# The last output tile of a gated cross-attention kernel, as one step of 288 rows or as two of 192 and 96

## The chip, the core and the metric

The kernel runs on one core of one Trainium2 chip. The metric is the device time of one execution in microseconds (us); the time of the kernel before is the median of three runs. A profile of one execution gives the rows that are read here. Its engines are PE (TensorE's matmuls), PEld (TensorE's weight loads), DVE (VectorE), ACT (ScalarE), POOL (GpSimd) and SP (SyncE, whose queue issues the DMAs).

## The reference

```python
# x (8, 100, 1024), memory (8, 722, 512), W_mem (1024, 512), W_gate (1024, 2048)
memory_proj = einsum('bme,de->bmd', memory, W_mem)
scores = einsum('bnd,bmd->bnm', x, memory_proj) / sqrt(1024)
attn = softmax(scores, axis=-1)
memory_context = einsum('bnm,bmd->bnd', attn, memory_proj)
gate_input = concatenate([x, memory_context], axis=-1)
gate = sigmoid(einsum('bnf,df->bnd', gate_input, W_gate) + b_gate)
fused = x + gate * memory_context
out = fused * rsqrt(mean(fused ** 2, axis=-1) + 1e-6) * norm_w
```

Eight batches of 100 rows make 800 rows of 1024 features. All is float32.

## The kernel before

Everything is kept with the feature on the partition and the row on the free axis, in eight tiles of 128 features (`KD` = 8). Products are made with fp32r operands split into a high and a low part: `three` (line 294) issues three matmuls for each pair of 128-feature tiles, high by high, low by high and high by low. Attention and the half of the gate product that needs only x come first. The stage that matters here is the last one: the gate product with the memory context, and what follows it.

That stage works through the list `STEPS`. A step is (output tile t, first row, end row): the first 512 rows of a tile (`FIRST`) or the last 288. The list runs the steps of 512 rows first, apart from one of 288 rows that stands third, and ends with seven steps of 288 rows, tiles 1 to 7. `END0` is the last step of 512 rows, `LAST` the last of all. For a step,

- PE runs `gate_mc(n)`: 8 input tiles by three matmuls into one of the PSUM banks 4 and 5 in turn. It first waits for the bank's seed, the x half of the gate product, which ACT writes there two steps ahead (`seed`);
- ACT takes the sigmoid with the bias (`sigmoid`, line 683), and in `finish` squares the fused tile (line 702) and multiplies it by norm_w (`weigh`, line 693);
- DVE multiplies by the memory context (`gate_times`, line 881), adds x (`fuse`, line 886), and adds the squares of the step before to the running sum (`sum_squares`, line 869). Between the steps it also scales the first 512 rows (`output`, line 898), which leave by DMA.

In ACT's loop `finish(n - 1)` stands behind the sigmoid of step n; for the last step it stands ahead of it.

The last 288 rows leave otherwise: as three chunks of 96 rows (`ROWS2`, `CHUNK`), transposed on PE so that a row lies on a partition. `turn(i, t0, t1)` (line 490) transposes tiles t0 to t1 of chunk i into a pair of PSUM banks, `TURN[i]`. Behind the last gate step PE turns seven tiles of chunks 0 and 1, waits for the square of the last tile (made on DVE, line 932), makes the mean of squares of all three chunks (lines 506 and 507), and turns the last tiles and all of chunk 2. DVE adds EPS (line 934), POOL takes the power -1/2 (line 954), ACT scales the left half of each chunk (line 722) and DVE the right half (line 938), and SP stores each chunk of 384 KB once both halves are there (line 282).

The order on each engine is written out by hand; the semaphores (`weighted`, `summed`, `late_squared`, `late_mean_made`, `late_rooted`, `turned`, `row_left`, `row_right`) hold the engines together.

Of the kernel before, what the change touches and what calls it, by code (L numbers as in the profile page):

```python
# [8 lines left out]
R = B * N  # L9
# [5 lines left out]
BANK = 512  # L15
# [5 lines left out]
ROWS2 = (R - FIRST) // CHUNK  # L21

TURN = ((0, 1), (2, 7), (4, 3))
# [9 lines left out]
    + [(t, FIRST, R) for t in range(1, KD)]  # L33
# [8 lines left out]
def build(nc, xT, ctxT, ctxN, w_mem, w_gate_x, w_mem_t, w_gate_mc, b_gate, norm_w, outT, out_rows):  # L42
# [4 lines left out]
    with top:  # L47
# [66 lines left out]
        def bank(i, cols, rows=P, at=0):  # L114
            return ps[0:rows, i * BANK + at:i * BANK + at + cols]
# [7 lines left out]
        def late_mean(i, n=1):  # L123
            return bank(6, n, CHUNK, 8 + i)
# [163 lines left out]
        def _(pe):  # L288
# [193 lines left out]
            def late_sums(i):  # L482
                at = FIRST + i * CHUNK
                return square_sum[:, at:at + CHUNK]
# [13 lines left out]
            for n in range(END0 + 4, LAST + 1):  # L498
                gate_mc(n)
            pe.wait_ge(weighted, LAST)  # L500
            turn(0, 0, KD - 1)
            turn(1, 0, KD - 1)
            pe.wait_ge(summed, LAST)
            pe.wait_ge(late_squared, 1)
            for i in range(ROWS2):
                nc.tensor.matmul(late_mean(i), late_sums(i), mean_w[:, :], start=True, stop=False)  # L506
                done = nc.tensor.matmul(late_mean(i), square[:, LAST % 2, i * CHUNK:(i + 1) * CHUNK], mean_w[:, :],
                                        start=False, stop=True)
            done.then_inc(late_mean_made, 1)
            pe.wait_ge(weighted, LAST + 1)  # L510
            turn(0, KD - 1, KD).then_inc(turned, 1)
            turn(1, KD - 1, KD).then_inc(turned, 1)
            pe.wait_ge(out_done, KD)
# [4 lines left out]
        def _(act):  # L518
# [188 lines left out]
            for n in range(LAST + 1):  # L707
                if n in SPLIT_AT:
                    split_gate_w(SPLIT_AT[n])
                if n == END0 + 1 or n == LAST:  # L710
                    finish(n - 1)
                sigmoid(n)
                if n + 2 <= LAST:
                    seed(n + 2)
                if n > 0 and n not in (END0 + 1, LAST):
                    finish(n - 1)
            act.wait_ge(late_squared, 1)
            weigh(LAST)
            for i in range(ROWS2):
                act.wait_ge(late_rooted, 1)  # L720
                act.wait_ge(turned, i + 1)
                nc.scalar.activation(row_out[:, i * D:i * D + BANK], bank(TURN[i][0], BANK, CHUNK), ACT.Copy,
                                     scale=rms_late[:, i:i + 1]).then_inc(row_left, 1)
# [3 lines left out]
        def _(dve):  # L727
# [199 lines left out]
            sum_squares(LAST - 1)  # L927
            gate_times(LAST)
            fuse(LAST)
            part = acc[:, KD - 1, FIRST:R]  # L930
            dve.wait_ge(fused, LAST + 1)
            nc.vector.tensor_tensor(square[:, LAST % 2, 0:R - FIRST], part, part, ALU.mult).then_inc(late_squared, 1)
            dve.wait_ge(late_mean_made, 1)
            nc.vector.tensor_scalar(rms_late[:, :], late_mean(0, ROWS2), EPS, None, ALU.add).then_inc(mean_copied, 1)
            for i in range(ROWS2):
                dve.wait_ge(late_rooted, 1)
                dve.wait_ge(turned, i + 1)
                nc.vector.tensor_scalar(row_out[:, i * D + BANK:(i + 1) * D], bank(TURN[i][1], BANK, CHUNK),  # L938
                                        rms_late[:, i:i + 1], None, ALU.mult).then_inc(row_right, 1)


        @block.gpsimd
        def _(pool):
# [9 lines left out]
            pool.wait_ge(mean_copied, 2)  # L953
            nc.gpsimd.tensor_tensor(rms_late[:, :], rms_late[:, :], minus_half[0:CHUNK, 0:ROWS2],
                                    ALU.pow).then_inc(late_rooted, 1)
# [30 lines left out]
```

## Time and profile before

| | |
|---|---|
| median of three runs | 303.08 us (302.94 to 303.28) |
| the profiled execution | 303.27 us, its span 301.5 us |
| PE busy | 292.5 us, 97% of the span |
| DVE, ACT busy | 166.5 us and 157.4 us, 55% and 52% |
| granted TensorE clock | 0.992 of full speed, mean over the span |
| DMA | 46.29 MB, mean 154 GB/s |

A busy time is the sum of the spans of an engine's instructions. A matmul's span runs from its start to the end of its result, and matmuls overlap: how fast they follow each other is read from start to start. The span begins with the first instruction and ends with the last; the rest of the execution's time lies around it.

### The profile page before, as it was taken

The page shows a single profiled execution, that of the slowest core. Times are in us where ns is not written, and L with a number is a line of the kernel's source. Part 1 is how long each engine was busy: PE and PEld are TensorE (multiplying, and loading weights), DVE is VectorE, ACT ScalarE, POOL GpSimd, SP SyncE. Part 2 cuts the span into 40 slices and gives each one's busy share as a digit, 9 for nine tenths or more (in the row PEclk, how much of TensorE's full clock was granted, in tenths as well). Part 3 has the DMA queues.
Part 4 walks back from the last instruction along what each step waited for, and adds up shares of the span by engine and source line. Part 5 has one row for each costly group of instructions (what it writes and reads, how often), then busy time and mean ns, then how long its engine had stood idle before and what let it go on. Part 6 is the DMA issues. An engine that isn't in the chain of part 4 may idle for free.

```text
span 301.5 us, 4214 instructions
## 1 busy us (share of the span) xinstructions
PE 292.5 (97%) x1647; PEld 272.2 (90%) x1647; DVE 166.5 (55%) x236; ACT 157.4 (52%) x231; POOL 2.6 (1%) x8
## 2 busy tenths in 40 slices
PE   8999999999999999999999999999999999999990
PEld 7999999898999989899898989999988888899980
DVE  2757564557575666756566534432365753444862
ACT  4648246464573836448373616454356845454542
POOL 0000000000000000000000000000000000001000
PEclk9999999999999999999999999999999999999996
DMA  6997291733928367372944011095123400000335
GB/s 208 408 385 244 94 339 56 238 115 111 277 89 316 136 199 262 105 257 102 299 161 150 13 70 40 29 340 236 70 72 136 143 2 0 1 0 2 139 141 157
DMA packets 18351, 46.29 MB, mean 154 GB/s; under 512 B 1520, under 2 KB 2288, under 8 KB 18336
## 3 DMA queue, kind: packets, MB, share of 16 engines
q1 hardware_dynamic: 18336, 46.09, 44.4%
q8 instruction: 10, 0.16, 0.2%
q14 instruction: 5, 0.04, 0.1%
HBM read 42.80 MB, written 3.28 MB: 153 GB/s over the span
## 4 chain that ended last, share of the span: by engine, by line
PE 96%; DMA 1%; DVE 1%; ACT 0%; DVEq 0%; issue 0%; ACTq 0%
PE ps L294 69%; PE ps L406 11%; PE ps L382 11%; PE ps L396 1%; PE ps L413 1%; DMA acc<-xT 1%; PE ps L319 0%; DVEq L47 0%; PE ps L490 0%; PE ps L322 0%; PE ps L325 0%; PE ps L478 0%; PE ps L470 0%; DVE x_again L938 0%; PE ps L506 0%
## 5 line engine op out<-in xcount | busy, mean ns | idle before, releaser
L294 PE MATMUL ps<-act_hi,w_hi 128*128 128x400 f32 (+2 forms) x268 | 79.4, 347 | 0.0
L294 PE MATMUL ps<-act_hi,w_lo 128*128 128x400 f32 (+2 forms) x268 | 78.7, 344 | 0.0
L294 PE MATMUL ps<-act_lo,w_hi 128*128 128x400 f32 (+2 forms) x268 | 78.7, 344 | 0.0
L294 PEld LDWEIGHTS ps<-act_hi,w_hi 128*128 128x128 f32 x268 | 49.2, 188 | 2.9
L294 PEld LDWEIGHTS ps<-act_lo,w_hi 128*128 128x128 f32 x268 | 49.8, 188 | 1.8
L294 PEld LDWEIGHTS ps<-act_hi,w_lo 128*128 128x128 f32 x268 | 49.8, 188 | 1.8
L729 DVE TENSOR_TENSOR w_lo<-w_stage,w_hi 128x1024 fp32r<-128x1024 f32 (+2 forms) x23 | 26.0, 1131 | 23.4 <-ACT w_hi L526 22.2
L729 DVE TENSOR_TENSOR cn_lo<-cn_stage,cn_hi 128x1536 fp32r<-128x1536 f32 (+2 forms) x24 | 28.5, 1217 | 5.2 <-ACT cn_hi L545 5.2
L729 DVE TENSOR_TENSOR ct_lo<-ct_stage,ct_hi 128x1444 fp32r<-128x1444 f32 x16 | 25.8, 1654 | 0.5 <-ACT ct_hi L537 0.5
L526 ACT ACTIVATE w_hi<-w_stage 128x1024 fp32r<-128x1024 f32 x20 | 21.0, 1054 | 7.9 <-PE ps L294 6.1
L621 ACT ACTIVATE pc<-ps,row_inv 100x512 f32<-100x512 f32 x8 | 5.5, 688 | 34.1 <-PE ps L406 34.1
L537 ACT ACTIVATE ct_hi<-ct_stage 128x1444 fp32r<-128x1444 f32 x16 | 21.7, 1409 | 0.0
L382 PE MATMUL ps<-ct_hi,qb_hi 128*100 128x362 f32 x64 | 21.4, 334 | 0.0
L605 ACT ACTIVATE probs<-ps,neg_top 100x722 f32<-100x722 f32 x8 | 6.9, 866 | 27.2 <-DVE neg_top L807 27.2
L382 PE MATMUL ps<-ct_hi,qb_lo 128*100 128x362 f32 x64 | 21.0, 328 | 0.0
L382 PE MATMUL ps<-ct_lo,qb_hi 128*100 128x362 f32 x64 | 21.0, 328 | 0.0
L683 ACT ACTIVATE gate<-ps,bias_t 128x288 f32<-128x288 f32 (+1 forms) x14 | 8.1, 579 | 24.2 <-PE ps L294 24.2
L881 DVE TENSOR_TENSOR gate<-gate,mc 128x512 f32<-128x512 f32 (+1 forms) x16 | 9.2, 573 | 20.0 <-ACT gate L683 20.0
L729 DVE TENSOR_TENSOR act_lo<-mc,act_hi 128x800 fp32r<-128x800 f32 x8 | 7.9, 993 | 20.5 <-ACT mc L654 20.5
L406 PE MATMUL ps<-cn_hi,pt_hi 128*100 128x512 f32 (+1 forms) x48 | 18.9, 394 | 0.0
L406 PE MATMUL ps<-cn_hi,pt_lo 128*100 128x512 f32 (+1 forms) x48 | 18.9, 393 | 0.0
L406 PE MATMUL ps<-cn_lo,pt_hi 128*100 128x512 f32 (+1 forms) x48 | 18.9, 393 | 0.0
(99 smaller groups left out, 447.1 us busy)
## 6 DMA issues: line engine op xcount, KB each, us to landing
ct_stage<-ctxT SPq DMA_DIRECT2D x16, 722.0 KB, 9.2
cn_stage<-ctxN SPq DMA_DIRECT2D x8, 768.0 KB, 5.4
cn_stage<-ctxN SPq DMA_DIRECT2D x8, 512.0 KB
w_stage<-w_gate_x SPq DMA_DIRECT2D x8, 512.0 KB, 7.9
w_stage<-w_gate_mc SPq DMA_DIRECT2D x8, 512.0 KB, 3.6
x_again<-xT SPq DMA_DIRECT2D x1, 3200.0 KB, 13.0
acc<-xT SPq DMA_DIRECT2D x6, 400.0 KB, 7.3
w_stage<-w_mem_t SPq DMA_DIRECT2D x4, 512.0 KB, 5.5
```

The costliest lines, as they stand in the source:

```text
L294: done = nc.tensor.matmul(o, wgt, stream[h][part], start=first and wgt is wh and part == 0, stop=last and wgt is wl, skip_group_check=onto)
L382: done = nc.tensor.matmul(bank(h, MH + 1, N), lhs[:, k, :], rhs[:, k, at:at + MH + 1], start=k == 0 and part == 0, stop=k == KC - 1 and pa ...
L396: done = nc.tensor.transpose(o, probs[:, t * P:t * P + rows], ident[0:N, 0:N])
L406: done = nc.tensor.matmul(bank(PCB, C, N), lhs[0:rows, t, :], rhs[0:rows, t, :], start=t == 0 and part == 0, stop=t == MT and part == 2)
L413: done = nc.tensor.transpose(bank(PTB5, N, P, c * N), pc[:, c * P:(c + 1) * P], ident[0:N, 0:N])
L526: nc.scalar.activation(w_hi[home][:, :], w_stage[:, slot, :], ACT.Copy).then_inc(w_hi_done, 1)
L537: nc.scalar.activation(ct_hi[:, 2 * s:2 * s + 2, :], ct_stage[:, 2 * s:2 * s + 2, :], ACT.Copy).then_inc(ct_hi_done, 1)
L605: nc.scalar.activation(probs[:, :].rearrange("p (h m) -> p h m", h=2), scores, ACT.Exp, bias=neg_top[:, :], scale=float(D) ** -0.5, accum_ ...
L621: nc.scalar.activation(pc[:, :], bank(PCB, C, N), ACT.Copy, scale=row_inv[:, :]).then_inc(pc_scaled, 1)
L683: nc.scalar.activation(part, part if n < 2 else gate_bank(n), ACT.Sigmoid, bias=bias_t[:, t:t + 1]).then_inc(gate_done, 1)
L729: return nc.vector.tensor_tensor(out, whole, hi.bitcast(F32), ALU.subtract)
L881: nc.vector.tensor_tensor(part, part, mc[:, t, r0:r1], ALU.mult).then_inc(gated, 1)
```

## The change

The last step, tile 7 with rows 512 to 799, becomes two: rows 512 to 703 (192) and rows 704 to 799 (96, from `LATE` on). The means of chunks 0 and 1 are taken from the sum of squares as soon as it holds the step of 192 rows, in a matmul each; that of chunk 2 waits for the square of the last 96 rows, which is made on DVE as before, and lies in PSUM bank 7 in place of bank 6. EPS and the power follow in two parts as well. PE turns each chunk whole, chunk 0 behind the first two means, chunk 1 behind chunk 2's mean, chunk 2 last. ACT does `finish` ahead of the sigmoid for both of the last steps.

```diff
-ROWS2 = (R - FIRST) // CHUNK
-TURN = ((0, 1), (2, 7), (4, 3))
+ROWS2, LATE = (R - FIRST) // CHUNK, R - CHUNK
+TURN = ((0, 1), (2, 3), (5, 4))
...
-    + [(t, FIRST, R) for t in range(1, KD)]
+    + [(t, FIRST, R) for t in range(1, KD - 1)] + [(KD - 1, FIRST, LATE), (KD - 1, LATE, R)]
...
-            return bank(6, n, CHUNK, 8 + i)
+            return bank(6, n, CHUNK, 8 + i) if i < ROWS2 - 1 else bank(7, n, CHUNK, BANK - 1)
...
+            pe.wait_ge(summed, LAST)
+            for i in range(ROWS2 - 1):
+                done = nc.tensor.matmul(late_mean(i), late_sums(i), mean_w[:, :], start=True, stop=True)
+            done.then_inc(late_mean_made, 1)
             pe.wait_ge(weighted, LAST)
-            turn(0, 0, KD - 1)
-            turn(1, 0, KD - 1)
-            pe.wait_ge(summed, LAST)
+            turn(0, 0, KD).then_inc(turned, 1)
             pe.wait_ge(late_squared, 1)
-            for i in range(ROWS2):
-                nc.tensor.matmul(late_mean(i), late_sums(i), mean_w[:, :], start=True, stop=False)
-                done = nc.tensor.matmul(late_mean(i), square[:, LAST % 2, i * CHUNK:(i + 1) * CHUNK], mean_w[:, :],
-                                        start=False, stop=True)
-            done.then_inc(late_mean_made, 1)
+            nc.tensor.matmul(late_mean(ROWS2 - 1), late_sums(ROWS2 - 1), mean_w[:, :], start=True, stop=False)
+            nc.tensor.matmul(late_mean(ROWS2 - 1), square[:, LAST % 2, 0:CHUNK], mean_w[:, :],
+                             start=False, stop=True).then_inc(late_mean_made, 1)
+            pe.wait_ge(out_done, KD)
+            turn(1, 0, KD).then_inc(turned, 1)
             pe.wait_ge(weighted, LAST + 1)
-            turn(0, KD - 1, KD).then_inc(turned, 1)
-            turn(1, KD - 1, KD).then_inc(turned, 1)
-            pe.wait_ge(out_done, KD)
             turn(2, 0, KD).then_inc(turned, 1)
...
-                if n == END0 + 1 or n == LAST:
+                early = n == END0 + 1 or n >= LAST - 1
+                if early:
                     finish(n - 1)
...
-                act.wait_ge(late_rooted, 1)
+                act.wait_ge(late_rooted, 1 + (i == ROWS2 - 1))
...
+            def late_mean_plus_eps(late, at, n):
+                dve.wait_ge(late_mean_made, late + 1)
+                nc.vector.tensor_scalar(rms_late[:, at:at + n], late_mean(at, n), EPS, None,
+                                        ALU.add).then_inc(mean_copied, 1)
+
             gate_times(LAST)
+            late_mean_plus_eps(0, 0, ROWS2 - 1)
             fuse(LAST)
-            part = acc[:, KD - 1, FIRST:R]
+            part = acc[:, KD - 1, LATE:R]
...
+            late_mean_plus_eps(1, ROWS2 - 1, 1)
+            for i in range(ROWS2):
+                right_half(i)
...
-            pool.wait_ge(mean_copied, 2)
-            nc.gpsimd.tensor_tensor(rms_late[:, :], rms_late[:, :], minus_half[0:CHUNK, 0:ROWS2],
-                                    ALU.pow).then_inc(late_rooted, 1)
+            for late, at, n in ((0, 0, ROWS2 - 1), (1, ROWS2 - 1, 1)):
+                pool.wait_ge(mean_copied, late + 2)
+                part = rms_late[:, at:at + n]
+                nc.gpsimd.tensor_tensor(part, part, minus_half[0:CHUNK, 0:n], ALU.pow).then_inc(late_rooted, 1)
```

How it stands on the engines. First PE's program from the end of the last gate matmuls on, before the change (ps is PSUM, mean_w the column of 1/1024, ident the identity; a shape is that of the result):

```order
L294 MATMUL ps<-act_hi,w_lo 128x288
L490 MATMUL ps<-ident,acc 96x128 [waits weighted]
L490 MATMUL ps<-ident,acc 96x128 x13
L506 MATMUL ps<-mean_w,square_sum 96x1 [waits late_squared,summed]
L507 MATMUL ps<-mean_w,square 96x1
...
L490 MATMUL ps<-ident,acc 96x128 [waits weighted]
L490 MATMUL ps<-ident,acc 96x128
L490 MATMUL ps<-ident,acc 96x128 [waits out_done]
L490 MATMUL ps<-ident,acc 96x128 x7
```

And with the change:

```order
L294 MATMUL ps<-act_hi,w_lo 128x192
L294 MATMUL ps<-act_hi,w_hi 128x96 [waits seeded,w_lo_done]
...
L294 MATMUL ps<-act_hi,w_lo 128x96
L502 MATMUL ps<-mean_w,square_sum 96x1 [waits summed]
L502 MATMUL ps<-mean_w,square_sum 96x1
L490 MATMUL ps<-ident,acc 96x128 [waits weighted]
L490 MATMUL ps<-ident,acc 96x128 x7
L507 MATMUL ps<-mean_w,square_sum 96x1 [waits late_squared]
L508 MATMUL ps<-mean_w,square 96x1
L490 MATMUL ps<-ident,acc 96x128 [waits out_done]
L490 MATMUL ps<-ident,acc 96x128 x7
L490 MATMUL ps<-ident,acc 96x128 [waits weighted]
```

Two of the three means now stand right behind the gate matmuls; of the 24 transposes, 8 stand ahead of the wait for the last square where 14 stood before, and 16 behind it.

Then DVE, from the last output of the first 512 rows on, as the difference:

```order
-L869 TENSOR_TENSOR square_sum<-square_sum,square 128x288 [waits summed,squared]
-L881 TENSOR_TENSOR gate<-gate,mc 128x288 [waits gate_done]
-L886 TENSOR_TENSOR acc<-gate,x_again 128x288 [waits gated]
-L932 TENSOR_TENSOR square<-acc 128x288 [waits fused]
...
+L869 TENSOR_TENSOR square_sum<-square_sum,square 128x192 [waits summed,squared]
+L881 TENSOR_TENSOR gate<-gate,mc 128x96 [waits gate_done]
+L930 TENSOR_SCALAR rms_late<-ps 96x2 [waits late_mean_made]
+L886 TENSOR_TENSOR acc<-gate,x_again 128x96 [waits gated]
+L938 TENSOR_TENSOR square<-acc 128x96 [waits fused]
+L930 TENSOR_SCALAR rms_late<-ps 96x1 [waits late_mean_made]
+L943 TENSOR_SCALAR x_again<-ps,rms_late 96x512 [waits turned,late_rooted] x3
```

The first addition of EPS stands between the product and the fuse of the last 96 rows, the second ahead of all three right halves.

## Rows read from the trace of the kernel before

**Rows 1.** The page: the span, and the busy time of each engine.
```profile
span 301.5 us, 4214 instructions
...
PE 292.5 (97%) x1647; PEld 272.2 (90%) x1647; DVE 166.5 (55%) x236; ACT 157.4 (52%) x231; POOL 2.6 (1%) x8
```

**Rows 2.** The chain that ended last, its end: start us, us, what.
```profile
275.93 14.02 PE ps L294 x105
293.30 1.15 PE ps L490 x10
...
295.86 0.66 DVE x_again L938
```

**Rows 3.** Timeline of the tail: start, us, engine, line, operation, [idle before].
```profile
286.56 0.30 PE L294 MATMUL ps<-act_hi,w_hi 128*128 128x288 f32 x1
...
288.83 0.54 ACT L693 ACTIVATE acc<-acc,norm_t 128x288 f32<-128x288 f32 x1
...
289.63 0.29 PE L294 MATMUL ps<-act_hi,w_lo 128*128 128x288 f32 x1
...
289.77 1.69 PE L490 MATMUL ps<-ident,acc 128*96 128x128 f32 x14
...
290.03 0.50 ACT L683 ACTIVATE gate<-ps,bias_t 128x288 f32<-128x288 f32 x1 [0.66 <-PE ps L294]
290.56 0.46 DVE L881 TENSOR_TENSOR gate<-gate,mc 128x288 f32<-128x288 f32 x1 [0.31 <-ACT gate L683]
...
292.15 0.30 PE L506 MATMUL ps<-mean_w,square_sum 128*96 128x1 f32 x2 [0.69 <-DVE square L932]
...
292.99 0.31 PE L507 MATMUL ps<-mean_w,square 128*96 128x1 f32 x2
...
293.34 0.16 DVE L934 TENSOR_SCALAR rms_late<-ps 96x3 f32<-96x3 f32 x1 [1.33 <-PE ps L507]
293.57 0.85 POOL L954 TENSOR_TENSOR rms_late<-rms_late,minus_half 96x3 f32<-96x3 f32 x1 [20.46 <-DVE rms_late L934]
...
294.46 2.06 DVE L938 TENSOR_SCALAR x_again<-ps,rms_late 96x512 f32<-96x512 f32 x3 [0.96 <-PE ps L490]
295.29 1.62 SPq L282 DMA_DIRECT2D out_rows<-x_again  x3
```

**Rows 4.** Stretches behind the first store's issue: busy by engine, PEclk, DMA share, GB/s.
```profile
296.10:297.60 1.50, 0.00 (x0) 0.00 (x0) 0.42 (x1) 0.19 (x1) 0.00 (x0) 0.73 1.01 276
297.60:299.10 1.50, 0.00 (x0) 0.00 (x0) 0.00 (x0) 0.00 (x0) 0.00 (x0) 0.50 1.01 320
299.10:300.60 1.50, 0.00 (x0) 0.00 (x0) 0.00 (x0) 0.00 (x0) 0.00 (x0) 0.50 0.56 191
```

**Rows 5.** The chain: pieces of 512, of 400 and of f32 128 columns.
```profile
141.67 4.17 PE ps L406 x18
...
151.45 4.35 PE ps L294 x24
...
275.04 0.89 PE ps L478 x8
```

**Rows 6.** Timeline, weight loads of 128 columns one behind the other.
```profile
274.74 0.99 PEld L478 LDWEIGHTS ps<-rms_diag,ones 128*128 128x128 f32 x8
```

**Rows 7.** Groups by shape, 245 to 302 us, ACT and DVE: busy, mean ns | idle.
```profile
L683 ACT ACTIVATE gate<-ps,bias_t 128x288 f32<-128x288 f32 x7 | 3.5, 499 | 9.6 <-PE ps L294 9.6
L689 ACT ACTIVATE ps<-acc 128x288 f32<-128x288 f32 x7 | 2.9, 416 | 0.2
L683 ACT ACTIVATE gate<-ps,bias_t 128x512 f32<-128x512 f32 x4 | 2.8, 690 | 11.0 <-PE ps L294 11.0
...
L689 ACT ACTIVATE ps<-acc 128x512 f32<-128x512 f32 x2 | 1.2, 602 | 0.1
...
L881 DVE TENSOR_TENSOR gate<-gate,mc 128x288 f32<-128x288 f32 x7 | 3.2, 457 | 5.3 <-ACT gate L683 5.3
L881 DVE TENSOR_TENSOR gate<-gate,mc 128x512 f32<-128x512 f32 x4 | 2.8, 692 | 12.2 <-ACT gate L683 12.2
```

More of the change, by code:

```diff
@@ L714, in _ @@
                     seed(n + 2)
-                if n > 0 and n not in (END0 + 1, LAST):
+                if n > 0 and not early:
                     finish(n - 1)
@@ L927, in _, with right_half @@
             sum_squares(LAST - 1)
+            def late_mean_plus_eps(late, at, n):
+                dve.wait_ge(late_mean_made, late + 1)
+                nc.vector.tensor_scalar(rms_late[:, at:at + n], late_mean(at, n), EPS, None,
+                                        ALU.add).then_inc(mean_copied, 1)
             gate_times(LAST)
+            late_mean_plus_eps(0, 0, ROWS2 - 1)
             fuse(LAST)
-            part = acc[:, KD - 1, FIRST:R]
+            part = acc[:, KD - 1, LATE:R]
             dve.wait_ge(fused, LAST + 1)
[L932 to L936, printed above, removed]
+            nc.vector.tensor_tensor(square[:, LAST % 2, 0:CHUNK], part, part, ALU.mult).then_inc(late_squared, 1)
+            def right_half(i):
+                dve.wait_ge(late_rooted, 1 + (i == ROWS2 - 1))
                 dve.wait_ge(turned, i + 1)
```

## The prediction

> **What bounds the kernel now.** I read the page first [rows 1]: TensorE (PE) is busy for 97% of the span, so only PE time or the tail behind PE's last product can move the end. The profiled execution took 303.27 us, with a span of 301.5 us; the other 1.8 us lie around the span and I leave them alone. It is the slowest of the three runs, 0.19 us above the median of 303.08. A measurement of this kernel can tell a difference of about 0.2%, 0.6 us, from none.
>
> Then the chain of waits [rows 2]: PE without a break up to the last gate step, then transposes, a wait, the last scaling on DVE, and after 296.52 only the stores. The timeline [rows 3] gives the tail link by link. The last gate step (24 matmuls of 288 columns) starts at 286.56 and starts its last matmul at 289.63. Sigmoid follows at 290.03, then three DVE passes from 290.56 on, the mean matmuls from 292.15 to the start of the last at 292.99, the addition of EPS at 293.34, the power on POOL at 293.57, the row halves at 294.46 and the first store's issue at 295.29.
>
> The stores bound what follows. In the stretches [rows 4] the DMA engines are full from 296.1 to 299.1 and 0.56 full for the next 1.5 us: 3.0 + 0.84 = 3.85 us of work, 1.28 us a store. It begins 0.8 us after the first issue. So the end hangs on the first store's issue, as long as the third store is ready before the first two are done.
>
> **Part 1: the narrow gate steps.** 24 matmuls of 288 columns become 24 of 192 and 24 of 96, each with its own weight load of 128 columns. This is the term everything depends on, and no fp32r matmul under 288 columns is in the trace. The last stretch of gate steps runs at 14.02 / 105 = 0.1335 us a matmul [rows 2]; at 512 columns it is 4.17 / 18 = 0.232 and at 400 columns 4.35 / 24 = 0.181 [rows 5]. That is a line of 0.44 ns a column. Carried on, it gives 0.091 us at 192 columns and 0.049 at 96. But a load must be done for each: eight loads of 128 columns stand at (0.99 - 0.19) / 7 = 0.114 us from start to start [rows 6], and the matmuls on them at 0.89 / 8 = 0.111 [rows 5]. Loads overlap the matmul ahead, so the longer of the two counts. I take 0.112 us for both widths, the row nearest in load and width. The last matmul of the 96-column step then starts at 286.56 + 47 x 0.112 = 291.82, against 289.63: **+2.19**. Bounds: the carried-on line from below, 0.133 (no cheaper than 288 columns) from above, and a much dearer end under the rivals.
>
> **Part 2: the passes behind it.** Sigmoid goes from 288 to 96 columns; 0.499 us at 288 and 0.690 at 512 [rows 7] give 0.336, so -0.16. The three DVE passes (times, fuse, square) are 0.457 at 288 and 0.692 at 512 [rows 7], so 0.256 at 96: -0.60. The last narrow matmul ends a little earlier after its start: -0.05. The first EPS addition now stands on DVE between the product and the fuse; between its 0.16 alone [rows 3] and nothing, if it overlaps, I take +0.10. Together **-0.71**.
>
> **Part 3: the means.** Before, 12 mean instructions (six f32 matmuls, two instructions each) are 0.84 / 10 = 0.084 apart [rows 3]. Now two matmuls for chunks 0 and 1 run behind the last gate step, while the passes run, and only two stay on the path: four instructions for twelve, **-0.67**.
>
> **Part 4: the power.** From the EPS addition at 293.34 to the first row half at 294.46 there are 1.12 us, mostly POOL's 0.85 [rows 3]. For chunk 0 the power now runs under the fuse and the square. But DVE's order puts the second EPS addition ahead of the first right half, so chunk 0's half still waits for the late square and the late means. It keeps about 0.1 of the 1.12: **-1.02**. ACT does the left half earlier, which is worth nothing, since SP waits for both halves.
>
> **Sum for the first store:** 2.19 - 0.71 - 0.67 - 1.02 = -0.21, an issue at about 295.1. So the change doesn't do what its words say: no chunk is stored while the third is made, because PE reaches the means only after the last narrow step.
>
> **The third store.** After the late means (last start about 293.82) PE has 16 transposes at 1.15 / 10 = 0.115 [rows 2], the last starting at 295.63 and landing at 295.9; before, 14 of 24 were done under the sigmoid. The second power, on POOL until about 295.3, is hidden under them. The third right half (0.74 us) ends at 296.69 and its store is issued at 296.78, 0.18 later than before. Its work could begin at 297.6; the first two stores hold the DMA engines until 295.9 + 2.57 = 298.5. So 0.9 us of cover are left, and the end follows the first store. If the third slipped by more than that, it would decide instead.
>
> **Other edits.** The seed of the last step is split in two on ACT, under a gate step. ACT's weighting of the step ahead ended at 289.37 [rows 3]; with one more seed (0.416 at 288 columns and 0.602 at 512 [rows 7], so 0.26 at 96) the 192-column sigmoid can start at 289.6 (its matmuls are ready at about 289.5), and its square and weighting, behind DVE's two passes, end at about 291.65. The last sigmoid is due at 292.17: 0.5 us of cover. The sum of squares that PE's first means wait for ends at about 291.55, 0.4 before PE gets there. The bank change for chunk 2's mean and the new pairs of banks for the transposes cost nothing: the outputs, which read bank 3, are done on DVE before the last step's passes begin. SP issues the same list.
>
> **Forecast:** 303.27 - 0.21 = 303.06 against the profiled execution, 302.87 against the median; I say 303.0.
>
> **Rivals.**
> (a) **Narrow fp32r matmuls run at the f32 rate; slower.** The four f32 matmuls of 128 columns at line 478 take eight instructions and 0.89 us [rows 5]: 0.2225 us each, 1.74 ns a column, against 0.46 for the fp32r ones of 288. The trace has fp32r only wide and f32 only narrow, so it can't say whether type or width sets the rate. For it: exactly this gap. Against: nothing shown ties a rate to a width. Then 192 columns take 0.334 us and 96 take 0.167: 24 x 0.334 + 23 x 0.167 = 11.86 instead of 5.26, all on PE ahead of the tail: +6.6, **309.7 us**. It decides once the mean spacing passes 0.129 us, where (0.129 - 0.112) x 47 = 0.8 eats the gain and 0.6 more.
> The Trainium skill (FP8 and Floating Point Precision, TensorE Precision Notes) says that true FP32 makes four passes, and lists a reduced-precision way that cuts FP32 inputs down; it ties neither to a width. By that rule type decides, rival (a) falls and 303.1 stands; the trace agrees with the ratio (1.74 to 0.46 ns), and doesn't show the width.
>
> (b) **The narrow stream doesn't cover the load**, so load and stream add up: 0.112 + 0.091 and 0.112 + 0.049. 24 x 0.203 + 23 x 0.161 = 8.6, +3.3: **306.4 us**. Against it: at 288 columns the spacing of 0.1335 is far below such a sum.
>
> (c) **The spacing stays at 0.133**, a floor of the instruction rather than of the columns: 47 x 0.021 = +1.0, **304.1 us**.
>
> (d) **Loads don't bind**, and the line goes on downwards; faster. PE would be done by 289.9, but then ACT holds: the last sigmoid can't start before 291.65, 0.5 earlier than forecast, so **302.5 us**, where ACT's order is the bound.
> The Trainium skill (TensorE: Matmul & The Clock Gate, Back-to-back issue gap) gives 81 ns a matmul for a sustained stream of load and matmul pairs at 128 columns. By that figure 47 x 0.081 = 3.8 would end PE 1.5 us before my forecast, and (d) would come out. The loads of 128 columns here stand 0.114 us apart, so the trace speaks against it for this type.
>
> **How the numbers follow.** Forecast within 0.2%: 0.40. (d) faster by over 0.2%: 0.12. (c), or a spacing near it: 0.08. (b): 0.05. (a): 0.35, high because nothing in the trace excludes it and the whole change rests on the unseen width. Faster 0.12, same 0.40, slower 0.48. The predicted time is that of the likeliest case, 303.0, whose own range is 302.5 to 304.1. For eight in ten the range must reach (a): 302.4 to 310.0.
>
> **What would show it.** In the new profile: the 192- and 96-column rows of line 294 and their spacing (0.112 right; 0.33 and 0.17 for (a)); PE at the means at 291.9; EPS additions at about 292.8 and 294.2; the first store issued at 295.1 and the third at 296.8; the DMA engines full from 295.9 for nearly 4 us. I am wrong if the spacing of either width is over 0.13 us, if ACT's sigmoid starts late with its matmuls long done, or if the end follows the third store.

## The result, and the profile after

The changed kernel took 302.16 us (median of 8 runs, 301.98 to 302.57) against 303.09 for the kernel before (8 runs), a ratio of 0.9972 with a 95% interval of 0.9963 to 0.9981. Measured once more beside its variants (run e8 below) it was 302.26 against 302.94, ratio 0.9982 (0.9973 to 0.9991). So it is faster, by 0.93 and by 0.68 us in the medians, and neither interval reaches 1. I had forecast no change, 303.0 us, and a range that ended at 302.4. Of the 11 executions of run e1 one was far off at 1659.89 us: it is in that run's median and not in its ratio; without it the median is 302.49.

The page of the changed kernel (span; busy time of each engine):

```profile
span 300.3 us, 4266 instructions
...
PE 293.7 (98%) x1667; PEld 272.8 (91%) x1667; DVE 167.2 (56%) x240; ACT 158.8 (53%) x235; POOL 3.0 (1%) x9
```

The profiled execution took 302.11 us. PE is busy 1.2 us longer and the span is 1.2 us shorter. The end of its chain of waits (start, us, what), which answers to [rows 2]:

```profile
275.42 16.11 PE ps L294 x129
...
292.88 0.33 PE ps L507 x2
293.21 0.17 PE ps L508 x2
293.38 1.81 PE ps L490 x16
...
295.28 0.75 DVE x_again L943
```

The power is gone from the chain; the 16 transposes of chunks 1 and 2 stand there. The chain runs over the third right half because the third store lands last; run e3 below shows that this doesn't make the third store the bound. The timeline of the changed kernel's tail, which answers to [rows 3]:

```profile
286.06 0.25 PE L294 MATMUL ps<-act_hi,w_hi 128*128 128x192 f32 x1
...
288.60 0.27 PE L294 MATMUL ps<-act_hi,w_lo 128*128 128x192 f32 x1
288.72 0.23 PE L294 MATMUL ps<-act_hi,w_hi 128*128 128x96 f32 x1
...
288.98 0.42 ACT L682 ACTIVATE gate<-ps,bias_t 128x192 f32<-128x192 f32 x1
...
291.24 0.28 PE L294 MATMUL ps<-act_hi,w_lo 128*128 128x96 f32 x1
...
291.61 0.34 ACT L682 ACTIVATE gate<-ps,bias_t 128x96 f32<-128x96 f32 x1 [0.54 <-PE ps L294]
...
291.99 0.26 DVE L881 TENSOR_TENSOR gate<-gate,mc 128x96 f32<-128x96 f32 x1 [0.97 <-ACT gate L682]
292.16 0.15 DVE L930 TENSOR_SCALAR rms_late<-ps 96x2 f32<-96x2 f32 x1
292.28 0.26 DVE L886 TENSOR_TENSOR acc<-gate,x_again 128x96 f32<-128x96 f32 x1
292.39 0.71 POOL L965 TENSOR_TENSOR rms_late<-rms_late,minus_half 96x2 f32<-96x2 f32 x1 [19.78 <-DVE rms_late L930]
292.57 0.26 DVE L938 TENSOR_TENSOR square<-acc 128x96 f32<-128x96 f32 x1
...
292.88 0.33 PE L507 MATMUL ps<-mean_w,square_sum 128*96 128x1 f32 x2 [0.15 <-DVE square L938]
...
293.42 0.15 DVE L930 TENSOR_SCALAR rms_late<-ps 96x1 f32<-96x1 f32 x1 [0.59 <-PE ps L508]
293.50 0.75 DVE L943 TENSOR_SCALAR x_again<-ps,rms_late 96x512 f32<-96x512 f32 x1
...
294.34 2.08 SPq L282 DMA_DIRECT2D out_rows<-x_again  x3
```

Both widths follow each other at the same pace: 23 spacings of the 192-column matmuls take 288.60 - 286.06 = 2.54 us, 0.110 each, and from the first 96-column one at 288.72 to the last at 291.24 it is 2.52, also 0.110. The power of chunks 0 and 1 runs on POOL beside the fuse and the square.

The two tails side by side, both from the first matmul of the (first) last step:

| us | before | after | difference | forecast |
|---|---|---|---|---|
| first to last gate matmul | 3.07 | 5.18 | +2.11 | +2.19 |
| to the first mean behind the last square | 2.52 | 1.64 | -0.88 | -0.71 |
| to the (last) EPS addition | 1.19 | 0.54 | -0.65 | -0.67 |
| to the first right half | 1.12 | 0.08 | -1.04 | -1.02 |
| to the first store's issue | 0.83 | 0.84 | +0.01 | 0 |
| to the end of the span | 6.21 | 5.96 | -0.25 | 0 |
| sum | 14.94 | 14.24 | -0.70 | -0.21 |

The span is printed to a tenth of a us, so the last stretch is good to 0.05; in the second profiles of both kernels (e12 and e8 below) the whole tail is 14.89 and 14.23 us, a difference of 0.66. Counted from the first matmul of the (first) last step, the three stores of the kernel before were issued at 8.73, 9.38 and 10.04 us and those of the changed kernel at 8.28, 9.17 and 10.04: the first 0.45 earlier, the second 0.21, the third at the same point. The second and the third store in the timeline, of the kernel before and then of the changed one (the first stands in [rows 3] and above):

```profile
295.94 0.33 SPq L282 DMA_DIRECT2D out_rows<-x_again  x1
...
296.60 0.32 SPq L282 DMA_DIRECT2D out_rows<-x_again  x1
```

```profile
295.23 0.33 SPq L282 DMA_DIRECT2D out_rows<-x_again  x1
...
296.10 0.32 SPq L282 DMA_DIRECT2D out_rows<-x_again  x1
```

The tail is worth about 0.7 us. The other 0.5 us between the two profiles lie far ahead of anything that the change touches. The chain of the kernel before, at its beginning:

```profile
5.34 0.67 PE ps L322 x2
...
42.74 3.98 PE ps L382 x24
```

And of the changed kernel:

```profile
6.37 0.36 PE ps L322 x2
...
42.24 3.98 PE ps L382 x24
```

The same pair of matmuls took 0.67 us in one execution and 0.36 in the other, and the chains are 0.5 us apart from there to the tail. The pair began 1 us later in the execution that came out ahead, so it wasn't an earlier start that put it ahead; the granted clock reads 1.00 in both stretches, and why the first matmuls ran at two paces stays open. In second profiles of both kernels (e8, e12) the last step began at 286.17 and 286.31, a difference of 0.14 instead of 0.50. Over all profiles of this case it began between 285.40 and 286.58 in the kernels with the two narrow steps, and between 285.60 and 286.56 in those with one step of 288 columns. So, as far as these profiles show, the difference in the start is chance, the tail is what the change does, and 0.70 agrees with both measured differences (0.93 and 0.68).

### The profile page after: what moved, and what is told of

Same layout as the page of the kernel before. It is cut to its first block, busy times and chain, and to the rows that moved or that the text cites. A ratio compares the mean times of both kernels' runs of the same rounds, so it can differ in the third digit from the quotient of the medians.

```text
span 300.3 us, 4266 instructions
## 1 busy us (share of the span) xinstructions
PE 293.7 (98%) x1667; PEld 272.8 (91%) x1667; DVE 167.2 (56%) x240; ACT 158.8 (53%) x235; POOL 3.0 (1%) x9
## 4 chain that ended last, share of the span: by engine, by line
PE 96%; DMA 1%; DVE 1%; SPq 0%; ACT 0%; issue 0%; DVEq 0%; ACTq 0%
PE ps L294 70%; PE ps L406 11%; PE ps L382 11%; PE ps L396 1%; DMA w_stage<-w_mem 1%; PE ps L413 1%; PE ps L490 1%; PE ps L478 0%; PE ps L470 0%; DVE x_again L943 0%; PE ps L319 0%; ACT w_hi L556 0%; SPq L232 0%; SPq L229 0%; PE ps L325 0%
## 5 line engine op out<-in xcount | busy, mean ns | idle before, releaser
L294 PE MATMUL ps<-act_hi,w_hi 128*128 128x400 f32 (+4 forms) x276 | 81.5, 344 | 0.0
L294 PE MATMUL ps<-act_hi,w_lo 128*128 128x400 f32 (+4 forms) x276 | 80.7, 342 | 0.0
L294 PE MATMUL ps<-act_lo,w_hi 128*128 128x400 f32 (+4 forms) x276 | 80.7, 342 | 0.0
L294 PEld LDWEIGHTS ps<-act_hi,w_hi 128*128 128x128 f32 x276 | 50.7, 188 | 3.2 <-DVE act_lo L729 0.2
L294 PEld LDWEIGHTS ps<-act_lo,w_hi 128*128 128x128 f32 x276 | 51.4, 188 | 1.8
L294 PEld LDWEIGHTS ps<-act_hi,w_lo 128*128 128x128 f32 x276 | 51.4, 188 | 1.8
L682 ACT ACTIVATE gate<-ps,bias_t 128x288 f32<-128x288 f32 (+3 forms) x15 | 8.4, 559 | 24.1 <-PE ps L294 24.1
L881 DVE TENSOR_TENSOR gate<-gate,mc 128x512 f32<-128x512 f32 (+3 forms) x17 | 9.3, 550 | 20.7 <-ACT gate L682 20.6
```

The source lines that it names most:

```text
L294: done = nc.tensor.matmul(o, wgt, stream[h][part], start=first and wgt is wh and part == 0, stop=last and wgt is wl, skip_group_check=onto)
L682: nc.scalar.activation(part, part if n < 2 else gate_bank(n), ACT.Sigmoid, bias=bias_t[:, t:t + 1]).then_inc(gate_done, 1)
L881: nc.vector.tensor_tensor(part, part, mc[:, t, r0:r1], ALU.mult).then_inc(gated, 1)
```

## The experiments

Two questions were open: what the narrow matmuls' spacing is made of, since all rested on it, and what the last 6 us behind the first store's issue hang on, since there 0.25 us came that no term of mine gave. The variants were measured in three groups, each beside the kernel before: e1 to e4 (303.02 us), e5 to e8 (302.94), and e9 to e12 (302.80). Across groups, compare the ratios.

**e1: chunk 0's right half ahead of the second EPS addition.**

```diff
-            late_mean_plus_eps(1, ROWS2 - 1, 1)
-            for i in range(ROWS2):
+            right_half(0)
+            late_mean_plus_eps(1, ROWS2 - 1, 1)
+            for i in range(1, ROWS2):
                 right_half(i)
```

> The changed kernel (302.16 us) with one exchange on DVE: chunk 0's right half ahead of the second EPS addition. Theory, the end follows the first store, because three stores keep the DMA engines full behind it: the half starts at 293.14 instead of 293.50 and the store is issued 0.36 us earlier, the third store at the same time as in the changed kernel, so about 301.8 us. Rival, the third store sets the end: nothing moves it (16 transposes hide the second power), 302.2 us.

Measured: 302.56 us, ratio to the kernel before 0.9983 (0.9974 to 0.9992); the changed kernel's was 0.9972 at first and 0.9982 in e8, so nothing was gained. The stores in the timeline (SP's queue; start, us to issue), one by one:

```profile
294.30 0.34 SPq L282 DMA_DIRECT2D out_rows<-x_again  x1
...
295.56 0.33 SPq L282 DMA_DIRECT2D out_rows<-x_again  x1
...
296.43 0.32 SPq L282 DMA_DIRECT2D out_rows<-x_again  x1
```

The last gate matmul started at 291.57 here, so the first store left 2.73 us behind it instead of 3.10: 0.37 earlier, as planned. From its issue to the span's end it took 6.50 us instead of 5.96. The second and the third store were issued where they were (3.99 and 4.86 us behind the last gate matmul). My theory of the end, on which the forecast stood, falls.

**e3: the third store later.** Chunk 2's right half is made twice, the first time into a spare place.

```diff
-            for i in range(ROWS2):
+            for i in range(ROWS2 - 1):
                 right_half(i)
+            dve.wait_ge(late_rooted, 2)
+            dve.wait_ge(turned, ROWS2)
+            nc.vector.tensor_scalar(spare, bank(TURN[2][1], BANK, CHUNK), rms_late[:, 2:3], None, ALU.mult)
+            right_half(ROWS2 - 1)
```

> The changed kernel with chunk 2's right half made twice, the first time into a spare place, so that the third store is issued about 0.7 us later and nothing else moves. Theory, the first store sets the end: 0 to +0.1 us, 302.2 us. Rival, the third store sets it: +0.7, 302.9 us.

Measured: 302.45 us, ratio 0.9980 (0.9971 to 0.9989). The third store was issued 1.54 us behind the second instead of 0.87, and the span ended 8.94 us behind the last gate matmul, against 9.06. The third store isn't the bound either: 0.67 us of delay cost nothing that the profile or the times show.

**e6: the second store later.** The same with chunk 1's half.

```diff
-            for i in range(ROWS2):
-                right_half(i)
+            right_half(0)
+            dve.wait_ge(late_rooted, 1)
+            dve.wait_ge(turned, 2)
+            nc.vector.tensor_scalar(spare, bank(TURN[1][1], BANK, CHUNK), rms_late[:, 1:2], None, ALU.mult)
+            right_half(1)
+            right_half(2)
```

> The changed kernel with chunk 1's right half made twice, so that the second store is issued 0.66 us later and the third, whose half queues behind it on DVE, 0.45 later. Theory, the chain over the stores passes through the second: 0.3 to 0.5 us slower than the changed kernel, about 302.6 us. Rival, only the first store's issue and the total work count: 302.2 us.

Measured: 302.74 us, ratio 0.9998 (0.9989 to 1.0007), on the chip where the changed kernel had 302.26: 0.48 slower, as expected of a chain that passes through the second store (9.62 us from the last gate matmul to the span's end instead of 9.06). The third store left 0.44 us later too, but e3 shows that this alone costs nothing.

**e5: the second store earlier too.**

```diff
+            pe.wait_ge(out_done, KD)
+            turn(1, 0, KD).then_inc(turned, 1)
             pe.wait_ge(late_squared, 1)
             nc.tensor.matmul(late_mean(ROWS2 - 1), late_sums(ROWS2 - 1), mean_w[:, :], start=True, stop=False)
             nc.tensor.matmul(late_mean(ROWS2 - 1), square[:, LAST % 2, 0:CHUNK], mean_w[:, :],
                              start=False, stop=True).then_inc(late_mean_made, 1)
-            pe.wait_ge(out_done, KD)
-            turn(1, 0, KD).then_inc(turned, 1)
...
-            late_mean_plus_eps(1, ROWS2 - 1, 1)
-            for i in range(ROWS2):
-                right_half(i)
+            right_half(0)
+            right_half(1)
+            late_mean_plus_eps(1, ROWS2 - 1, 1)
+            right_half(2)
```

> The changed kernel with chunk 1 served earlier too: PE turns chunk 1 ahead of the late mean of chunk 2, and DVE makes the right halves of chunks 0 and 1 ahead of the second EPS addition. From the profiles so far a store that has the engines to itself is done 2.7 us after its issue, and one that queues behind another about 1.3 us after that one. Theory, the end is a chain over all three stores, so that an earlier first store alone (run e1) leaves a hole ahead of the second: now the first is issued 0.36, the second 0.58 us earlier, the third 0.1 later, and the last is done 0.4 earlier, about 301.8 us. Rival, the third store's issue sets the end: 302.2 to 302.3 us.

Measured: 302.15 us, ratio 0.9973 (0.9963 to 0.9983), the changed kernel beside it 0.9982 (0.9973 to 0.9991). The issues moved as planned (by -0.37, -0.62 and -0.02 against the last gate matmul); the end moved by 0.14 (8.92 instead of 9.06). The direction is that of the chain, the size a third of it, and the times can't tell 0.14 from nothing.

**e8 and e12: both kernels again.**

> The changed kernel again, on the same chip as its variants and with a second profile. If the shorter drain behind the first store (4.38 us from the first packet to the last one's end, against 4.61 before) belongs to the spacing of the stores and not to chance, it comes out within 0.05 us of 4.38 again; the time 302.1 to 302.3 us.

> The kernel before again, for a second profile: if its drain is no chance it comes out within 0.05 us of 4.61 us, and the stretch from the last gate step's first matmul to the span's end within 0.1 of 14.94 us; the start of that step may move by some tenths, as the first loads and the clock do.

Measured: e8 302.26 us, its drain (from the start of the first DMA packet of the stores to the end of the last, in the trace) 4.36 us; e12, a single execution, 303.00 us, drain 4.60, and from the last step's first matmul to the span's end 14.89 us. With 4.38 and 4.61 in the first profiles, the two drains came out again within 0.02 us.

**e11: the spacing alone.** The kernel before, with a small scaling (`SPARE` = 160 columns) ahead of the second and third right half.

```diff
                 dve.wait_ge(turned, i + 1)
+                if i > 0:
+                    nc.vector.tensor_scalar(spare[:, (i - 1) * SPARE:i * SPARE], bank(TURN[i][1], SPARE, CHUNK), rms_late[:, i:i + 1], None,
+                                            ALU.mult)
```

> The kernel before with a scaling of 160 columns into a spare place ahead of the second and of the third right half, which delays the second store by about 0.24 us and the third by about 0.48, the first not at all: the spacing of the changed kernel without its change. Theory, the spacing of the stores sets how fast they drain: 4.4 us from the first packet to the last one's end instead of 4.61, so the kernel ends 0.2 us earlier although two of its stores leave later, 302.9 us against 303.1. Rival: later stores end later or at the same time, 303.1 to 303.5 us.

Measured: 302.72 us against 302.80, ratio 0.9997 (0.9988 to 1.0006): a gain of 0.2 us is too small to be seen in these times, and not excluded. The one profile shows it. Stores of e11:

```profile
294.53 0.34 SPq L284 DMA_DIRECT2D out_rows<-x_again  x1
...
295.46 0.33 SPq L284 DMA_DIRECT2D out_rows<-x_again  x1
296.41 0.32 SPq L284 DMA_DIRECT2D out_rows<-x_again  x1
...
DMA to landing us min/median/max: 3.0/3.4/3.7
```

The span is 300.5 us and the last gate matmul started at 288.86: 11.64 us to the end, against 11.87 and 11.82 in the two profiles of the kernel before, with the second store 0.29 and the third 0.58 us later. Its drain is 4.40 us. The line on landing (from a store's issue to its end) for the kernel before is this:

```profile
DMA to landing us min/median/max: 3.1/3.8/4.5
```

All runs by the spacing of their stores; the drain is from the first packet's start to the last one's end:

| run | gaps between issues | drain | first issue to span's end |
|---|---|---|---|
| before / e12 | 0.65, 0.66 / 0.65, 0.65 | 4.61 / 4.60 | 6.21 / 6.16 |
| e2 | 0.64, 0.66 | 4.62 | 6.16 |
| e5 | 0.64, 1.47 | 4.57 | 6.19 |
| e7 | 0.71, 0.75 | 4.50 | 6.05 |
| after / e8 | 0.89, 0.87 | 4.38 / 4.36 | 5.96 / 5.95 |
| e10 (below) | 0.89, 0.87 | 4.48 | not comparable, PE's added matmuls end last |
| e11 | 0.93, 0.95 | 4.40 | 5.97 |
| e3 | 0.89, 1.54 | 4.29 | 5.84 |
| e1 | 1.26, 0.87 | 4.90 | 6.50 |
| e6 | 1.54, 0.66 | 4.98 | 6.52 |
| e4 / e9 | 1.62, 0.65 | 4.98 / 4.99 | 6.58 / 6.57 |

Among these runs a gap of about 0.9 ahead of the second store drains best. Shorter ones cost 0.1 to 0.2 us, longer ones 0.5 to 0.6. The same gaps gave 4.36, 4.38 and, in e10, 4.48 us, so what the spacing explains is 0.1 to 0.25 us. Two stretches near the end of the drain (columns as in [rows 4]), first of the kernel before, then of the changed kernel:

```profile
299.25:300.15 0.90, 0.00 (x0) 0.00 (x0) 0.00 (x0) 0.00 (x0) 0.00 (x0) 0.50 0.72 241
300.15:301.00 0.85, 0.00 (x0) 0.00 (x0) 0.00 (x0) 0.00 (x0) 0.00 (x0) 0.50 0.11 39
```

```profile
298.30:299.20 0.90, 0.00 (x0) 0.00 (x0) 0.00 (x0) 0.00 (x0) 0.00 (x0) 0.50 0.68 250
299.20:300.05 0.85, 0.00 (x0) 0.00 (x0) 0.00 (x0) 0.00 (x0) 0.00 (x0) 0.50 0.03 10
```

By the packets of the trace, the last moment with 15 or more engines busy lies 1.40 and 1.32 us ahead of the drain's end in the two profiles of the kernel before, and 0.85 and 0.83 us ahead of it in those of the changed one: with short gaps the engines are full without a dip and then finish unevenly. With a gap of 1.54 us ahead of the second store (e6) they run short in between:

```profile
295.70:296.15 0.45, 0.00 (x0) 0.00 (x0) 0.11 (x1) 0.00 (x0) 0.00 (x0) 1.00 0.39 146
```

**e2: the split without the rest.** PE's two narrow steps stay; means, EPS and power follow in one piece behind the last square (chunk 2's mean lies in bank 6 again; ACT's and DVE's waits, left out here, follow).

```diff
-            pe.wait_ge(summed, LAST)
-            for i in range(ROWS2 - 1):
-                done = nc.tensor.matmul(late_mean(i), late_sums(i), mean_w[:, :], start=True, stop=True)
-            done.then_inc(late_mean_made, 1)
             pe.wait_ge(weighted, LAST)
             turn(0, 0, KD).then_inc(turned, 1)
             pe.wait_ge(late_squared, 1)
+            pe.wait_ge(summed, LAST)
+            for i in range(ROWS2 - 1):
+                nc.tensor.matmul(late_mean(i), late_sums(i), mean_w[:, :], start=True, stop=True)
...
-            late_mean_plus_eps(0, 0, ROWS2 - 1)
...
-            late_mean_plus_eps(1, ROWS2 - 1, 1)
+            late_mean_plus_eps(0, 0, ROWS2)
...
-            for late, at, n in ((0, 0, ROWS2 - 1), (1, ROWS2 - 1, 1)):
+            for late, at, n in ((0, 0, ROWS2),):
```

> The changed kernel's gate steps of 192 and 96 rows, but the means of all three chunks, EPS and the power in one piece behind the last square. Theory, as in my sum: against the changed kernel four more mean instructions (+0.34) and the power back on the path (+1.04), so 302.16 + 1.4 = 303.5 us, slower than the kernel before. Rival, the transposes of chunks 1 and 2 would have hidden means and power anyway: 302.5 us.

Measured: 303.72 us, ratio 1.0025 (1.0016 to 1.0034). The first store left 4.49 us behind the last gate matmul instead of 3.10: +1.39, where the sum gave 0.34 + 1.04 = 1.38. Its drain is the kernel before's (4.62 us, gaps of 0.64 and 0.66). So the split alone is a loss, and the early means, the power out of the way and the gaps between the stores that come with them turn it into the gain.

**e10: what the 0.11 us are.** Behind the last transpose, seven groups of 12 fp32r matmuls.

```diff
+            pe.wait_ge(late_rooted, 2)
+
+            def rate(held, cols):
+                for k in range(12):
+                    nc.tensor.matmul(bank(6, cols, held), act_hi[:, k % KD, 0:held], act_lo[:, k % KD, 0:cols],
+                                     start=True, stop=True)
+
+            for held, cols in ((128, 96), (128, 192), (128, 224), (128, 256), (64, 96), (64, 192), (32, 96)):
+                rate(held, cols)
```

> The changed kernel with seven groups of 12 fp32r matmuls behind PE's last transpose, into a bank that nothing reads any more; weights of 128, 64 or 32 columns, streams of 96 to 256. It shows what the 0.112 us of both narrow widths are. Theory, the weight load: with 128 held, 96, 192 and 224 columns all stand about 0.112 apart and 256 about 0.119; with 64 held, 96 columns about 0.06 and 192 about 0.09; with 32 held, 96 columns about 0.05. Rival, a floor of the instruction: 0.112 with 64 and 32 held too.

Measured in one execution, groups of e10 by shape (128*64: 64 columns held; the last shape is the stream; busy us, mean ns of one):

```profile
L518 PE MATMUL ps<-act_lo,act_hi 128*128 128x256 f32 x12 | 1.6, 280 | 0.0
L518 PE MATMUL ps<-act_lo,act_hi 128*128 128x192 f32 x12 | 1.5, 278 | 0.0
L518 PE MATMUL ps<-act_lo,act_hi 128*128 128x96 f32 x12 | 1.5, 276 | 0.0
L518 PE MATMUL ps<-act_lo,act_hi 128*128 128x224 f32 x12 | 1.5, 276 | 0.0
L518 PE MATMUL ps<-act_lo,act_hi 128*64 128x192 f32 x12 | 1.2, 252 | 0.0
L518 PE MATMUL ps<-act_lo,act_hi 128*64 128x96 f32 x12 | 0.8, 221 | 0.0
L518 PE MATMUL ps<-act_lo,act_hi 128*32 128x96 f32 x12 | 0.7, 207 | 0.0
```

(Busy less one matmul) / 11 is the spacing, to about 0.005 us: 0.11 for all widths up to 224 with 128 columns held, 0.12 at 256, but 0.086 (192 columns) and 0.053 (96) with 64 held, 0.045 with 32 held. From start to start in the trace the two with 64 held stand 0.089 and 0.058 apart. The width of the stream doesn't set 0.11, nor does a floor of the instruction; the load of 128 columns does. All seven groups are fp32r, so the type isn't varied here.

**e4: no narrow steps, only the passes split.** PE keeps the 288-column step; ACT, DVE, means and power serve the first 96 rows, then the other 192. `means` and `late_eps` make the means and add EPS for a range of chunks; the second EPS addition stands between the first and the second right half.

```diff
+EPS_AHEAD_OF = 1
+HEAD = 1
+PIECES = ((FIRST, FIRST + HEAD * CHUNK), (FIRST + HEAD * CHUNK, R))
...
+            means(0, HEAD)
             pe.wait_ge(weighted, LAST + 1)
...
+            turn(2, 0, KD - 1)
+            pe.wait_ge(late_squared, 2)
+            means(HEAD, ROWS2)
+            pe.wait_ge(weighted, LAST + 2)
+            for i in range(HEAD, ROWS2):
+                turn(i, KD - 1, KD).then_inc(turned, 1)
...
+            for late, (a, b) in enumerate(PIECES):
+                part, whole = gate[:, LAST % 2, a - FIRST:b - FIRST], acc[:, KD - 1, a:b]
+                dve.wait_ge(gate_done, LAST + 1 + late)
+                nc.vector.tensor_tensor(part, part, mc[:, KD - 1, a:b], ALU.mult).then_inc(gated, 1)
+                dve.wait_ge(gated, LAST + 1 + late)
+                nc.vector.tensor_tensor(whole, part, x_again[:, KD - 1, a:b], ALU.add).then_inc(fused, 1)
+                if late == 1:
+                    late_eps(0)
+                dve.wait_ge(fused, LAST + 1 + late)
+                nc.vector.tensor_tensor(square[:, LAST % 2, a - FIRST:b - FIRST], whole, whole,
+                                        ALU.mult).then_inc(late_squared, 1)
             for i in range(ROWS2):
+                if i == EPS_AHEAD_OF:
+                    late_eps(1)
```

> The kernel before with its gate step of 288 columns kept whole on PE; only what follows is split, into 96 rows and 192 rows (sigmoid, product, fuse, square, mean, EPS, power, weighting), so nothing is paid for narrow matmuls. Theory, the narrow steps cost 2.1 us and the gain comes from the shorter passes and from the power off the path: the first store comes 1.4 us earlier than in the changed kernel, the third about 0.8 earlier, so about 300.9 us. Rival, the second piece of 192 rows queues behind the first on DVE and its stores set the end: about 302.0 us.

Measured: 301.74 us, ratio 0.9959 (0.9945 to 0.9973), faster than the kernel before, but 0.8 short of the theory. Against the changed kernel it is ahead by the ratio (0.9972 and 0.9982 there), though the intervals touch, and by the profile: 13.62 us from the step's first matmul to the span's end instead of 14.24. The timeline of e4:

```profile
292.44 0.25 PE L509 MATMUL ps<-mean_w,square_sum 128*96 128x1 f32 x2
...
293.25 0.15 DVE L952 TENSOR_SCALAR rms_late<-ps 96x2 f32<-96x2 f32 x1
...
293.48 0.70 POOL L989 TENSOR_TENSOR rms_late<-rms_late,minus_half 96x2 f32<-96x2 f32 x1 [0.93 <-DVE rms_late L952]
294.21 1.26 ACT L743 ACTIVATE x_again<-ps,rms_late 96x512 f32<-96x512 f32 x2 [0.95 <-POOL rms_late L989]
```

The second power isn't hidden here (ACT and DVE wait 0.95 and 0.81 us for it), and the second store leaves 1.62 us behind the first: the drain goes up to 4.98 us.

**e9: e4 with its second means ahead of chunk 2's transposes.**

```diff
-            pe.wait_ge(out_done, KD)
-            turn(2, 0, KD - 1)
             pe.wait_ge(late_squared, 2)
             means(HEAD, ROWS2)
             pe.wait_ge(weighted, LAST + 2)
-            for i in range(HEAD, ROWS2):
-                turn(i, KD - 1, KD).then_inc(turned, 1)
+            turn(1, KD - 1, KD).then_inc(turned, 1)
+            pe.wait_ge(out_done, KD)
+            turn(2, 0, KD).then_inc(turned, 1)
```

> Run e4 (gate step whole, 96 rows served first, then 192) with PE's seven transposes of chunk 2 moved from ahead of the means of chunks 1 and 2 to behind them. In e4 those means start 0.3 us after the late square is there, because PE is still turning. Theory: second and third store are issued 0.25 us earlier, the first as before, the hole between the first and the second store's ends shrinks by as much: about 301.5 us. Rival: the end depends on the first store alone or on the total work, 301.7 us.

Measured: 301.66 us, ratio 0.9959 (0.9946 to 0.9973), and all three stores where they were in e4. The timeline of e9 says why:

```profile
292.50 0.75 DVE L970 TENSOR_SCALAR x_again<-ps,rms_late 96x512 f32<-96x512 f32 x1 [0.45 <-POOL rms_late L988]
292.64 0.31 PE L510 MATMUL ps<-mean_w,square 128*96 128x1 f32 x2
...
293.17 0.15 DVE L951 TENSOR_SCALAR rms_late<-ps 96x2 f32<-96x2 f32 x1
```

The means are done at about 292.95, where e4's were done at 293.21 (3.58 and 3.76 us behind the last gate matmul), but DVE is at chunk 0's right half until about 293.2, and adds EPS 3.80 us behind the last gate matmul in both runs. Once PE no longer held the means back, DVE did.

**e7: e4 with the 192 rows first.**

```diff
-HEAD = 1
+HEAD = 2
```

> As run e4 (gate step whole, what follows in two pieces), with the 192 rows first and the 96 rows second, so that two stores can leave early. The first store is issued about 0.5 us later than in e4, the second and third 0.3 to 0.4 earlier. Theory, the chain over the stores: e4 lost 1.9 us between its first and second store's ends, here 1.3, so about the same end as e4, 301.7 us. Rival, the first store decides: 302.2 us.

Measured: 301.74 us, ratio 0.9965 (0.9953 to 0.9978): 0.5 us less than the changed kernel beside it, 302.26, and the same median as e4, as expected. Its first store leaves 0.81 us later than e4's against the last gate matmul, more than I had thought, the second 0.10 earlier and the third at the same time; the drain of 4.50 us instead of 4.98 gives back 0.5 of it. In the profiles e7 takes 13.90 us from the step's first matmul to the span's end, e4 13.62: the 0.3 between them don't show in the times.

## Why the prediction was wrong

- **The step that failed** is the last term of the sum: the stretch behind the first store's issue, which I took as fixed (0.8 us and then 3.85 us of work for the DMA engines, "the end follows the first store") and so put at no change. It measured -0.25 us. The drain itself depends on the gaps between the stores, and the change moved the first of them from 0.65 to 0.89 us. The first store was to come 0.21 us earlier and came 0.45 earlier; the end moved by 0.70. e1 shows the rule false (first store 0.37 earlier, end no earlier), e3 that the third doesn't decide, e6 that the second's delay costs, and e11 gets the shorter drain out of the kernel before with nothing but a delay, in one profile. I had the three stores' issue times in the forecast and read only the first. None of the signs of being wrong that I had named came out; this was not among them.
- **The passes** (Part 2) were mis-sized: -0.88 instead of -0.71. The EPS addition, for which I took +0.10, cost nothing. The fuse starts 0.29 us behind the product, as the square does behind the fuse, although the addition stands between them, and in e2, without the addition there, the fuse starts 0.30 behind the product: it fills the time in which the fuse would wait. PE reached its first mean behind the square 0.31 us after the square's start, where it took 0.60 before: the shorter square explains 0.20 of that, and the other 0.09 I had not counted.
- **The narrow steps** (Part 1) were right. 0.112 us for both widths came out at 0.110, +2.11 instead of +2.19. Of the rivals (a), the f32 rate with a chance of 0.35, is refuted: 192 columns don't take 0.334 us nor 96 columns 0.167, and e10 shows that up to 224 columns the load of 128 columns decides. (b), which needs 0.203 and 0.161, and (c), which needs 0.133, are refuted by the same 0.110. (d) falls too: the kernel is faster, but PE ended at 291.24 and not at 289.9, and ACT's last sigmoid waited 0.54 us for it.
- **What rival (a) rested on** was weaker than it looked. Each of the eight f32 instructions of line 478 loads 128 columns, and e10 shows that such a load alone takes 0.11 us; so their 0.111 us, read as 1.74 ns a column, can't tell the type's rate from the load's, nor is the ratio to 0.46 ns shown to be that of four passes. The Trainium skill (FP8 and Floating Point Precision, TensorE Precision Notes) ties neither of its two ways for FP32 to a width, and here the spacing didn't rise in the narrow steps. The Trainium skill's 81 ns a matmul (TensorE: Matmul & The Clock Gate, Back-to-back issue gap) isn't reached here with 128 columns held: 110 ns.
- **The means and the power** (Parts 3 and 4) were right to 0.02 us each, and e2 puts them back: 1.39 us against 1.38. That the change stores no chunk while the third is made was right: the first store's issue is at 294.34, 3.1 us behind the last gate matmul.
- **The range** ended at 302.4 because its low end was the bound of the one term in Part 1, cut off by ACT's order. What came in addition, 0.08 us from Part 1, 0.17 from Part 2 and 0.25 from the drain, all had the same sign, and the last two had no bound of their own.
- **The distance in all** is 0.84 us, from 303.0 to 302.16. Those three terms are 0.50 of it. Another 0.13 is my rounding up: against the median my own sum gave 302.87. The rest, about 0.2, is the part of the first measured 0.93 that the tail of 0.70 doesn't hold; two measurements of the same pair differ by as much (0.93 and 0.68).

Still open is why three stores 0.65 us apart drain 0.2 us slower than 0.9 apart. The packets' mean was 214 ns before and 208 after, which is 0.11 us of work an engine (3.85 and 3.74); the other half of the 0.23 is time in which engines stand idle. What makes either so, no run shows.

## What to carry to other kernels

A split of a step costs PE the weight loads, not the columns: with 128 columns held, an fp32r matmul of 96 to 224 columns is no cheaper than 0.11 us, where one of 288 takes 0.1335. So split the passes behind the product before the product itself (e7 beat the change by 0.5 us beside it, and e4 did as well as e7). Where several stores end a kernel, neither the first nor the last need set the end alone (e1, e3): forecast all the issue times, and look at the gaps. An instruction put into the wait between two dependent ones on the same engine can be free, as the EPS addition was on DVE.

## What the runs showed of the hardware that was not expected

- Three stores of 384 KB took 4.29 to 4.99 us from first packet to last, for the same 3.7 to 3.9 us of packet time an engine, mostly by the gaps between their issues (the same gaps differed by up to 0.12 us); in its one profile, two later stores made e11's tail 0.2 us shorter, which its times don't resolve.
- The spacing of fp32r matmuls went by the longer of load and stream: about 0.11 us with 128 columns held for 96, 192 and 224 columns streamed, 0.058 with 64 held and 96 streamed, 0.089 with 64 held and 192 streamed (e10, one execution).
- POOL's power took 0.55 to 0.60 us for one column of 96 rows, about 0.70 for two and 0.85 for three, by the profile, whose spans on POOL are rough.
